# A fused attention and mixture-of-experts layer in fp32: scores, values and outputs of a batch four steps later, its stacking transfers in another order, and the rows of maxima sent from ScalarE's queue

## The reference

```python
kv_c = rmsnorm(xn @ W_kv) * g_kv ; q_c = xn @ W_q
q = concat(q_c @ W_qdec, rope(q_c @ W_qrope))      # 16 heads of 8 + 32
k = concat(kv_c @ W_kdec, rope(xn @ W_krope))
attn = softmax(causal(q k^T / sqrt(40)))           # 256 x 256 for each head
attention = (attn @ (kv_c @ W_vdec)) @ W_o
cw = top-2 weights of softmax(xn @ Wg), 8 experts of width 512
experts = sum_e cw_e * (silu(xn @ W1_e + b1_e) @ W2_e + b2_e) + 0.1 * shared(xn)
```

## Time and profile before

| | before |
|---|---|
| median of 3 runs | 901.26 us (900.87 to 902.4) |
| the profiled execution, its own time | 900.5 us |
| its span, first to last instruction | 898.8 us |
| mean granted TensorE clock | 0.917 |
| bytes moved by DMA | 141.60 MB, mean 158 GB/s |

### The profile page before, as it was taken

How to read it: one execution, slowest core, us unless ns; L and a number is a source line. 1 busy time by engine, 2 the same in 40 slices (tenths; PEclk the granted TensorE clock), 3 DMA queues, 4 the chain that set the end, 5 groups by cost and what they waited for, 6 DMA issues and landing times.

```text
span 898.8 us, 14676 instructions
## 1 busy us (share of the span) xinstructions
PE 680.9 (76%) x4646; PEld 534.1 (59%) x4646; DVE 606.3 (67%) x1632; ACT 392.7 (44%) x842; POOL 289.3 (32%) x284
## 2 busy tenths in 40 slices
PE   0447877688786878778877787776636999999996
PEld 0335665566564656556665566555524788888885
DVE  3447578676768867657786575774672577778996
ACT  0112343343433434434343343433304677778773
POOL 5432322425345252232322223226100000046674
PEclk9998699898988999989898898988958899999998
DMA  5245534456455454352332524425108677789863
GB/s 156 83 157 182 179 130 158 155 165 193 138 163 165 142 183 131 100 165 91 118 125 97 168 93 122 138 86 175 33 13 257 194 229 252 242 269 295 280 178 102
DMA packets 66053, 141.60 MB, mean 158 GB/s; under 512 B 9035, under 2 KB 34616, under 8 KB 65976
## 3 DMA queue, kind: packets, MB, share of 16 engines
q1 hardware_dynamic: 61879, 132.26, 46.0%
q0 software_dynamic: 4096, 8.40, 3.4%
HBM read 47.30 MB, written 29.88 MB: 86 GB/s over the span
## 4 chain that ended last, share of the span: by engine, by line
PE 43%; DVE 20%; issue 12%; SPq 9%; DMA 8%; POOL 4%; ACT 3%; POOLq 0%; DVEq 0%; ACTq 0%
PE bank L1577 7%; SPq L474 6%; DMA QK<-mT 5%; PE bank L1595 4%; DVE heads_low L992 4%; POOL QK L700 3%; PE bank L1409 3%; DVE mx L983 3%; PE bank L1422 3%; PE bank L1342 3%; PE bank L1359 3%; ACT heads_high L720 2%; PE bank L1599 2%; PE bank L1425 2%; PE bank L1345 2%
## 5 line engine op out<-in xcount | busy, mean ns | idle before, releaser
L983 DVE TENSOR_REDUCE mx<-bank 128x3 f32<-128x384 f32 x256 | 142.0, 555 | 158.5 <-PE bank L1425 157.6
L738 ACT ACTIVATE prob<-bank 128x384 f32<-128x384 f32 x256 | 125.0, 490 | 155.8 <-PE bank L1345 154.7
L1422 PE MATMUL bank<-QK 120*128 120x256 f32 x256 | 102.0, 398 | 95.1 <-issue 66.7
L647 POOL TENSOR_TENSOR rot<-rot,t 128x512 f32<-128x512 f32 x64 | 81.7, 1277 | 270.6 <-DVE t L975 270.6
L700 POOL DMA_INDIRECT QK<-expert_outs,out_at x64 | 66.0, 1032 | 190.6 <-DMA expert_outs<-prob 172.0
L1422 PEld LDWEIGHTS bank<-QK 120*128 120x128 f32 x256 | 55.0, 215 | 108.5 <-issue 71.3
L1285 DVE TENSOR_TENSOR QK<-vaug,QK 128x512 fp32r<-128x512 f32 x124 | 86.5, 699 | 38.5 <-ACT QK L829 35.9
L720 ACT ACTIVATE heads_high<-bank 120x384 fp32r<-120x384 f32 x128 | 62.9, 491 | 107.1 <-PE bank L1409 106.5
L1342 PE MATMUL bank<-QK 122*128 122x256 f32 x256 | 92.5, 361 | 22.6 <-DMA QK<-mT 22.6
L992 DVE TENSOR_TENSOR heads_low<-bank,heads_high 120x384 fp32r<-120x384 f32 x128 | 70.8, 553 | 28.7 <-ACT heads_high L720 28.2
L1409 PE MATMUL bank<-ident,rot 128*120 128x128 f32 x384 | 70.0, 296 | 12.6 <-DVE heads_low L992 9.7
(11 more groups left out here) (222 smaller groups left out, 1424.9 us busy)
## 6 DMA issues: line engine op xcount, KB each, us to landing
QK<-heads_high SPq DMA_DIRECT2D x128, 200.0 KB
wb<-weight_parts SPq DMA_DIRECT2D x46, 512.0 KB, 4.9
QK<-heads_high SPq DMA_DIRECT2D x64, 240.0 KB
QK<-heads_low SPq DMA_DIRECT2D x64, 200.0 KB
weight_parts<-wb SPq DMA_DIRECT2D x18, 512.0 KB, 4.9
QK<-heads_low SPq DMA_DIRECT2D x32, 240.0 KB
rot<-expert_rows SPq DMA_DIRECT2D x23, 256.0 KB, 4.4
expert_outs<-prob SPq DMA_DIRECT2D x23, 256.0 KB, 4.7
```

The source lines that it names most:

```text
L738: act_f(prob[:, h % P_SLOTS, :], ST_PS[h % 2][:, P:4 * P], ACT.Exp, scale=SCALE).then_inc(s_exp, 1)
L983: V.tensor_reduce(mx[:, 0:3, h], B_PS[bank_of(k)][:, 0:3 * P].rearrange("p (a c) -> p a c", a=3), AX.X, ALU.max).then_inc(s_bfree[bank_of( ...
L1422: mm(ps[:, 0:T], q[:, P:T], kk, start=True, stop=False, skip_group_check=True)
```

## The change

Five tables, four step numbers and the constants `SHIFT` and `MAX_AT` move the maxima, the scores, the values and the output steps of a batch four steps later. The preparation, the projections, the turning and the router keep their steps. SyncE's program loses both `place_max`, and `restack` of q2 stands behind k0. ScalarE issues the two transfers of maxima itself, after a wait for its own copy.

```diff
-SHIFT = 2
-MAX_AT = 6
+SHIFT = 6
+MAX_AT = 10
...
-MROWS_AT = {14: (1, 0), 6: (0, 1)}
-PV_AT = {7: (0, 0), 11: (0, 1), 15: (0, 2), 3: (1, 3)}
-READ_AT = {12: (0, 0), 4: (1, 1)}
-BACK_AT = {13: (0, 0), 5: (1, 1)}
-NORMED_AT = {14: (0, 0), 6: (1, 1)}
-TURN_STEP, PUT_STEP, WO_STEP, ADD_STEP = 7, 8, 9, 10
+MROWS_AT = {2: (0, 0), 10: (0, 1)}
+PV_AT = {11: (0, 0), 15: (0, 1), 3: (1, 2), 7: (1, 3)}
+READ_AT = {0: (1, 0), 8: (1, 1)}
+BACK_AT = {1: (1, 0), 9: (1, 1)}
+NORMED_AT = {2: (1, 0), 10: (1, 1)}
+TURN_STEP, PUT_STEP, WO_STEP, ADD_STEP = 11, 12, 13, 14
...
-            def place_max(beta, half):
-
-                sp.wait_ge(s_mT, 2 * beta + half + 1)
-                sp.dma_start(QK[KQ:KK, beta % 2, 0, half * GH:(half + 1) * GH, :].bitcast(F32),
-                             mT[:, half, :].bitcast(F32)).then_inc(s_mrow[half], 16)
...
-                if known(b):
-                    place_max(b, 0)
-                if known(b + 1):
-                    restack(b + 1, "q", 2)
...
-                    for i in range(3):
-                        restack(b + 1, "k", i)
-                if known(b):
-                    place_max(b, 1)
+                    restack(b + 1, "k", 0)
+                    restack(b + 1, "q", 2)
+                    restack(b + 1, "k", 1)
+                    restack(b + 1, "k", 2)
...
                 act_f(mT[:, half, :], B_PS[bank_of(k)][0:2 * GH, 0:T], ACT.Copy).then_inc(s_mT, 1)
+                sc.wait_ge(s_mT, 2 * beta + half + 1)
+                sc.dma_start(QK[KQ:KK, beta % 2, 0, half * GH:(half + 1) * GH, :].bitcast(F32),
+                             mT[:, half, :].bitcast(F32)).then_inc(s_mrow[half], 16)
```

## The result

| | before | after |
|---|---|---|
| median of the runs | 901.7 us | 880.46 us (874.83 to 882.25) |
| ratio, 95% interval | | 0.9744 [0.9692, 0.9796] |
| profiled run, its span | 900.5, 898.8 us | 874.83, 873.1 us |

The change makes the kernel 2.6% faster. The forecast was 822 us in a range of 788 to 858, so the direction was right and the size was not. Of the 78 us forecast, the medians gained 21.2 and the profiled execution, the fastest of its three, 25.7. One more execution of the changed kernel took 955.19 us at a mean granted clock of 0.717, against 0.915 to 0.923 in the three used here.

A forecast was written before the change was run, and what follows sets the result against it. Neither TensorE (76% busy) nor VectorE (67%) fills the span; TensorE's waits were the missing time. -67 us over 14 turns, +8 router, -7 - 8 + 4 - 8 outside made -78 us, so 822 us, range 788 to 858.

The forecast's parts named there:

- The wait for k0 in step 6: TensorE's wait before the first maximum of the next batch; k0 four steps ahead of its reader ends it, -3.9 us a turn.
- forecast 8: First routed pass: SyncE, without maxima in its queue, zeroes rows and issues loads while `list_blocks` runs, -8 us.
- forecast 7 + 8 - 4 = 11: Outside the 14 turns: first batch's longest wait -7 us, turn 14's waits and slow clock -8, longer drain +4.
- ScalarE's two issues: Transfers of maxima on ScalarE: +0.2 us a turn, bound 3.2; rival with ScalarE held there, 850 us, chance 0.12.
- the small stacks: Step 2: five VectorE instructions now stand ahead of `small_stacks`, +0.6 us a turn, bounds 0 and 1.1.
- the wait ends: TensorE's wait at the scores for the rows of maxima, moved to ScalarE's queue, goes: -1.6 us a turn.
- +0.7 each: TensorE's waits for VectorE's negated maxima at steps 2 and 10: +1.4 us a turn together, bounds 0 and 1.7 each.
- +1.0: ScalarE's high part at step 8 waits for q2, which lands late: +1.0 us a turn, bounds 0 and 3.
- -1.5: The slow clock behind TensorE's stand-still for k0 goes: -1.5 us a turn, 1.7 at most.
- -3.9 - 1.5 - 1.6 - 1.0 + 1.4 + 0.6 + 0.2 + 1.0 = -4.8 us: Per turn: k0, clock, maxima's rows, step 14's VectorE wait, negated maxima, small stacks, ScalarE's issues, q2; -67 us for 14 turns.
- The rival of the ring of two banks: TensorE, ScalarE and VectorE share two banks, so waits move to VectorE: 1.5 us more a turn, 843 us, chance 0.18.
- the 2 of the forecast: Four router turns: VectorE has 29.11 us of work, not 24.05, formerly hidden by waits; +2 us each, +8 in all.

The follow-up runs named there:

- the run with the bank first: Changed kernel with VectorE's head_max of step 2 ahead of the small products and the normalisation: 878.36 us, 0.9751 of the kernel before.
- the run with the negation first: Changed kernel with VectorE negating the maxima at the end of steps 1 and 9, ahead of small products and normalisation: 918.0 us, 0.9797 of the kernel before.
- The split kernel: Changed kernel with each stacking transfer of 40 rows issued as two, of 32 and 8 rows: 0.9815 of the kernel before.
- step 7 without q2: Changed kernel with negated maxima at steps 3 and 11, first scores at step 7, q2's transfers left out from batch 2 on: 0.9456 of the kernel before.

## Why the prediction was wrong

**Right.** The wait for k0 in step 6 is gone, and so is TensorE's wait for the first rows of the expert part. What follows the last head's scores is 10.9 us shorter (forecast 8). First batch, turn 14 and drain together gave 67.3 - 57.3 - 2.1 = 7.9 us (forecast 7 + 8 - 4 = 11). ScalarE's two issues cost 0.62 us each and nothing that shows, and the small stacks cost nothing that shows: TensorE's wait for `qs` fell from 10.6 to 7.5 us. Each new wait stands where I had put it: steps 2, 8 and 10.

**Wrong: "the wait ends", at the maxima's rows.** I took 3.2 us from issue to reader from one transfer. In the changed kernel it is 5.55 us, and only 9.3 of the 22.6 us went. Two of the runs bear on it. ScalarE issuing in the old schedule:

```profile
380.99 3.55 SPq L468 DMA_DIRECT2D QK<-heads_high  x2
...
381.79 0.62 ACTq L720 DMA_DIRECT2D QK<-mT  x1
...
387.62 0.39 PE L1335 MATMUL bank<-QK 122*128 122x256 f32 x1 [0.39 <-DMA QK<-mT]
```

And SyncE issuing in the new one:

```profile
361.84 1.32 SPq L463 DMA_DIRECT2D QK<-mT  x1
...
367.07 0.40 PE L1343 MATMUL bank<-QK 122*128 122x256 f32 x1 [2.34 <-DMA QK<-mT]
```

That is 5.83 and 5.23 us, so in the new schedule it is not ScalarE's queue that makes the trip long. Nor is it how much the DMA engines carried, 188 GB/s during the trip of 3.2 us and 139 during that of 5.55:

```profile
385.39:388.56 3.17, 1.37 (x12) 1.03 (x11) 1.76 (x6) 1.33 (x3) 0.00 (x0) 1.00 0.53 188
```

```profile
413.56:419.11 5.55, 5.16 (x40) 3.97 (x39) 3.49 (x16) 2.25 (x6) 2.69 (x3) 0.69 0.45 139
```

What makes 3.2 us or 5.5 of the same transfer stays open.

**Wrong: "+0.7 each" for the negated maxima.** 3.5 us a turn and not 1.4, just over the upper bound of 3.4. I priced the wait for VectorE's negation. At step 2 it is the bank of PSUM that L1427 waits for, released by a maximum that stands behind the small products and the normalisation (the run with the bank first takes 23.5 us of it away, the run with the negation first none). At step 10 it is VectorE's own program of steps 9 and 10, not q2: the wait is 45.9 - 21.4 = 24.5 us in the changed kernel and 26.0 without q2. At step 11 it is gone (the 13.5 us that the kernel with later maxima keeps stand at step 3).

**Wrong: "+1.0" for q2, and more than its size.** The wait is 2.0 us. Without q2 the turn is 1.5 and 1.9 us shorter where q2 leads the chain, and no shorter where the rows of maxima do. I worked out a queue of 2.18 MB that starts at step 0. But q2 can't start before the last score of step 5, and what counts is a chain: that score, the issues, 5.42 us of trip, 7.7 us in all for the steps 6 and 7 and what of step 8 lies ahead of ScalarE's high part. The split kernel changed two of these, the trip and the issues, in opposite directions, and their sum hardly moved.

**Wrong: "-1.5" for the low clock.** The mean granted clock of the turns stayed 0.91. The stand-still of 3.7 us left, and several of 1.4 to 2.4 us came. Behind the 2.37 us that ended at 389.78 the clock fell, and it was at its lower level for 6 us, in which the wait of 1.39 us before 392.89 lies:

```profile
391.00:397.00 6.00, 4.61 (x25) 3.10 (x27) 2.96 (x9) 1.67 (x5) 2.24 (x2) 0.50 0.25 78
```

The three kernels with the shortest turns (later maxima, q2 left out, and step 7 without q2) have 0.93.

**The step that failed** is thus the sum itself, "-3.9 - 1.5 - 1.6 - 1.0 + 1.4 + 0.6 + 0.2 + 1.0 = -4.8 us": it subtracts waits from the turn one by one. The turn fell by 0.5 us. TensorE's idle time in the turns was 118.4 us before and 119.4 after, and it is 481.45 - 393.30 = 88.2 in the kernel whose turns without router reach the forecast. TensorE, ScalarE and VectorE hand on two banks, and two transfers of some 5 us stand in that ring. I read the chains above so that the turn is as long as the longest path through it; they and the table fit this, but no sum over such a path was worked out against the runs. The rival of the ring of two banks named this, and gave it 1.5 us a turn; it took 3.5 (36.2 us for a turn without router, against 32.7). The router's turns are 39.1 us, 2.9 above the others, where the trace before has 0.4 (37.8 and 37.4): 2.5 more, near the 2 of the forecast.

ScalarE did not stand still at its issues. All 32 issues of ScalarE together (min, median, max):

```profile
L720 ACTq DMA_DIRECT2D QK<-mT x32: 621/622/1236, 85.6 to 658.0; - x32
```

In the run with ScalarE's issue alone, the one at 381.79 (above) took 0.62 us while SyncE was in two issues of 3.55 us together, begun at 380.99. SyncE had taken 0.68 and 1.59 us for the same transfer. By the rule of the Trainium skill, "Perfetto Trace Analysis", section "DMA Instruction — HWDGE (DVE, Sync)", a lock wait would show in these durations; the first of the 32 is 0.62 us over the shortest and the others at most 0.03, so no wait of the length of SyncE's issues shows here.

## To carry to other kernels

In a pipeline of in-order engines over few buffers, don't subtract waits: take the chain of work over some turns, cross out its largest item and ask which chain is the next longest. For each transfer in the ring, count from the event that allows it (here the last reader of what it overwrites) to its reader, with its trip as measured at that place, and compare with the steps between. A shift of the schedule gives to one transfer what it takes from another; here the gain of the expert part was had by the queue alone, and the maxima one step later (steps 3 and 11) gave 15.5 us more (882.26 to 866.77) beside the 20 of the whole change on the same chip.

## What the runs showed of the hardware

- The same small transfer of maxima took 3.2 us from issue to reader in one kernel and 5.55 us in the other, as long as q2's last part with 5.42, which carries far more bytes. From SyncE's queue in the new schedule it took 5.23 us, and the rate was higher during the short trip (188 against 139 GB/s).
- Transfers of 40 rows split into 32 and 8 rows kept the DMA engines busier (share 0.63 against 0.43 over 14 turns) and moved no more bytes a second (139 against 140 GB/s). The last one's trip fell from 5.41 to 3.51 us.
- ScalarE's issues took 0.62 us in the median, and the one shown took that within two issues of SyncE of 3.55 us together.
- One chip ran the kernel before in 937.16 us, the others in 901 to 902.5; so only ratios to it on the same chip are compared.
